# Attention stage: q before k in the transposes of a tile, and P normalized by ScalarE before it is transposed

## The reference, cut to what matters

```python
h = shift_token(x)
q, k, v = split(h @ wqkv, 3)                 # 4096 x 512 each
q = l2norm(q) * q_scale;  k = l2norm(k) * k_scale
q, k = rotary_xpos(q, k)
# every token sees the tokens of the last 256 places (window of three tiles)
sim  = (8 * q) @ k.T, masked                 # per head, 128 x 384 for a tile
attn = softmax(sim)                          # exp, row sum, divide
o    = attn @ v
x    = x + o @ wo
```

## Time and profile before

| | us |
|---|---|
| median of 3 runs | 3535.35 (3533.59 to 3536.51) |
| the profiled execution | 3534.11 |
| its span, first to last instruction | 3532.3 |
| PE busy, of the span | 3269.6 (93%) |
| DVE busy | 1825.5 (52%) |
| ACT busy | 1227.1 (35%) |
| POOL busy | 937.7 (27%) |
| attention stages, by the 64 reciprocals (L1184) | from 354 to 1104 and from 1977 to 2729 |

### The profile page before, as it was taken

How to read it: one execution, slowest core, us unless ns; L and a number is a source line. 1 busy time by engine, 2 the same in 40 slices (tenths; PEclk the granted TensorE clock), 3 DMA queues, 4 the chain that set the end, 5 groups by cost and what they waited for, 6 DMA issues and landing times.

```text
span 3532.3 us, 53670 instructions
## 1 busy us (share of the span) xinstructions
PE 3269.6 (93%) x19880; PEld 2666.5 (75%) x19880; DVE 1825.5 (52%) x3534; ACT 1227.1 (35%) x2445; POOL 937.7 (27%) x1536
## 2 busy tenths in 40 slices
PE   5995999999995999999996899999998799999999
PEld 5884777777774888787774777777776578777787
DVE  2553666666665443333333566666666534333343
ACT  1112555555553111111112555555554211111111
POOL 0004555455454300000001554554553600000000
PEclk9997999999998999999998999999999899999999
DMA  3223111111113211111113101111111411111110
GB/s 115 72 72 130 55 58 55 61 52 37 58 49 91 69 60 60 60 54 60 60 60 130 49 31 60 58 55 60 58 46 52 114 60 60 60 60 60 60 60 30
DMA packets 167415, 225.26 MB, mean 64 GB/s; under 512 B 25032, under 2 KB 94792, under 8 KB 166904
## 3 DMA queue, kind: packets, MB, share of 16 engines
q1 hardware_dynamic: 150264, 205.06, 17.7%
q10 hardware_dynamic: 16896, 16.78, 1.5%
HBM read 131.60 MB, written 60.83 MB: 54 GB/s over the span
## 4 chain that ended last, share of the span: by engine, by line
PE 76%; issue 7%; POOL 7%; DVE 6%; ACT 2%; DMA 1%; SPq 1%; POOLq 0%; DVEq 0%; ACTq 0%
PE bank L311 25%; PE bank L313 23%; PE bank L312 23%; PE bank L694 3%; PE bank L504 2%; POOL a_rt L1421 1%; DVE a_ss L1136 1%; POOL a_rs L1422 1%; POOL a_rt L1419 1%; POOL a_rt L1418 1%; DVE a_V_lo L1164 1%; ACT a_sq L883 1%; PE bank L758 1%; DMA a_stage<-in_L_ffn_wqkv 1%; DVE a_krot L1143 1%
## 5 line engine op out<-in xcount | busy, mean ns | idle before, releaser
L311 PE MATMUL bank<-f_hT_hi,f_w_hi 128*128 128x512 f32 (+1 forms) x1408 | 560.4, 398 | 15.6 <-ACT f_hT_hi L992 15.6
L313 PE MATMUL bank<-f_hT_hi,f_w_lo 128*128 128x512 f32 (+1 forms) x1408 | 558.0, 396 | 0.0
L312 PE MATMUL bank<-f_hT_lo,f_w_hi 128*128 128x512 f32 (+1 forms) x1408 | 557.3, 396 | 0.0
L1332 DVE SCALAR_TENSOR_TENSOR f_uraw<-bank,f_b,f_gate 128x512 f32<-128x512 f32 (+1 forms) x176 | 132.1, 751 | 721.4 <-ACT f_gate L1008 721.2
L1008 ACT ACTIVATE f_gate<-bank,f_b 128x512 f32<-128x512 f32 (+1 forms) x176 | 121.2, 689 | 1008.3 <-PE bank L313 1008.3
L922 ACT ACTIVATE a_P<-a_S,a_bias 128x384 f32<-128x384 f32 x512 | 314.6, 615 | 304.1 <-DVE a_bias L1177 304.1
L1188 DVE TENSOR_TENSOR a_PT_lo<-bank,a_PT_hi 128x768 fp32r<-128x768 f32 x256 | 244.4, 955 | 236.5 <-ACT a_PT_hi L927 236.5
L311 PEld LDWEIGHTS bank<-f_hT_hi,f_w_hi 128*128 128x128 f32 (+1 forms) x1408 | 261.1, 185 | 80.4 <-ACT f_hT_hi L992 16.2
L311 PE MATMUL bank<-a_PT_hi,a_V_hi 128*64 128x128 f32 x1536 | 301.8, 232 | 15.1 <-DVE a_PT_lo L1188 10.7
L313 PEld LDWEIGHTS bank<-f_hT_hi,f_w_lo 128*128 128x128 f32 (+1 forms) x1408 | 261.6, 186 | 67.7
L312 PEld LDWEIGHTS bank<-f_hT_lo,f_w_hi 128*128 128x128 f32 (+1 forms) x1408 | 261.5, 186 | 66.5
(11 more groups left out here) (168 smaller groups left out, 6998.7 us busy)
## 6 DMA issues: line engine op xcount, KB each, us to landing
a_h<-x_layer_in SPq DMA_DIRECT2D x128, 128.0 KB, 2.2
a_res<-x_layer_in SPq DMA_DIRECT2D x64, 256.0 KB, 2.8
x_after_attention<-out_tiles SPq DMA_DIRECT2D x64, 256.0 KB, 2.0
f_h<-x_after_attention ACTq DMA_DIRECT2D x32, 512.0 KB, 4.4
f_res<-x_after_attention SPq DMA_DIRECT2D x64, 256.0 KB, 3.6
f_x<-in_x SPq DMA_DIRECT2D x64, 256.0 KB, 3.6
x_layer_in<-f_res SPq DMA_DIRECT2D x64, 256.0 KB, 2.9
out<-f_res SPq DMA_DIRECT2D x64, 256.0 KB, 3.0
```

Of the source, the lines that this page charges most:

```text
L311: pe.matmul(dst, w[0], m[0], start=start, stop=False)
L312: pe.matmul(dst, w[0], m[1], start=False, stop=False)
L313: return pe.matmul(dst, w[1], m[0], start=False, stop=stop)
L1332: dve.scalar_tensor_tensor(f_uraw[0:ROWS[m], m % 2, :], bank[pair_of(u, m)][0:ROWS[m], :], f_b1[0:ROWS[m], 0, m:m + 1], f_gate[0:ROWS[m], ...
```

## The change

The P of a head is multiplied by its reciprocal row sum on ACT right after the exponential and before its transposes (`normalize`, in place, two heads at a time), in four portions per tile. DVE makes the reciprocals in four portions of two heads (`inverse(x, i)`), into a buffer of two tiles. The widening on POOL, the transposes of the reciprocals on PE, their copy on ACT and the multiplication of PV on DVE are gone. `o_hi` and `o_lo` now read PV from PSUM, in two halves of 64 partitions each.

The transposes of q go to slot B (`q_T`), those of k to slot C (`k_T`); the buffer of the transposed q is doubled, because the next tile's q is now written while the scores of the tile still read it. POOL rotates q ahead of the norms. The orders of ACT and DVE are written anew to match. In addition the transposes wait for other readers of their bank.

```diff
-            a_QT = pair(s, "a_QT", [P, PAIRS, P])
+            a_QT = pair(s, "a_QT", [P, 2, PAIRS, P])
-            a_inv = s("a_inv", [P, H])
+            a_inv = s("a_inv", [P, 2, H])
-            a_inv_wide = s("a_inv_wide", [P, H, HD])
-            a_invT = s("a_invT", [P, PAIRS, P])
-            a_O = s("a_O", [P, PAIRS, P])
 # tensor
+                def q_T(x):
+                    pe.wait_ge(a_q_rotated, START + G + x + 1)
+                    if here(x + 1):
+                        pe.wait_ge(a_hT_lo, START + G + x + 2)
+                    transpose_tile(turn, a_qrot[:]).then_inc(a_QT_mm, 1)
                 def k_T(x):
                     pe.wait_ge(a_k_normed, START + G + x + 1)
-                    if x >= 2:
-                        pe.wait_ge(a_invT_set, START + G + x - 1)
-                    else:
-                        pe.wait_ge(a_hT_lo, START + G + x + 2)
+                    pe.wait_ge(a_QT_hi, START + G + x + 1)
+                    pe.wait_ge(a_QT_lo, START + G + x + 1)
                     transpose_tile(turn, a_krot[:]).then_inc(a_KT_mm, 1)
-                def inv_T(x): ...
                 def p_T(x, i):
-                    pe.wait_ge(a_exp, START + (G + x) * H + 2 * i + 2)
+                    pe.wait_ge(a_P_set, START + (G + x) * H + 2 * i + 2)
                 # step: slot A
-                    if here(t - 1):
-                        inv_T(t - 1)
                 # slot B
-                        k_T(t + 1)
+                        q_T(t + 1)
                 # slot C
-                        q_T(t + 1)
+                        k_T(t + 1)
 # scalar
                 def o_hi(x):
-                    act.wait_ge(a_O_set, START + (G + x + 1) * 2)
-                    act.activation(a_OT[0][:], a_O[:], ACT.Copy).then_inc(a_O_hi, 1)
+                    act.wait_ge(a_PV_mm, START + (G + x + 1) * PAIRS)
+                    for odd in range(2):
+                        act.activation(a_OT[0][odd * HD:odd * HD + HD, :, :], quarters(bank[4 + odd][0:HD, :]), ACT.Copy)\
+                           .then_inc(a_O_hi, 1)
+                def normalize(x, i):
+                    act.wait_ge(a_inv_set, START + (G + x) * PAIRS + i + 1)
+                    for h in (2 * i, 2 * i + 1):
+                        act.activation(a_P[:, h % 4, :], a_P[:, h % 4, :], ACT.Copy, scale=a_inv[:, x % 2, h:h + 1])\
+                           .then_inc(a_P_set, 1)
 # order on ACT after the change:
 # square(0,t+1) q_copy(t+1) exp(t,2) o_hi(t-1) p_T(t,0) exp(t,3) normalize(t,1) value(t+1)
 # exp(t,4) exp(t,5) p_T(t,1) q_T(t+1) normalize(t,2) exp(t,6) exp(t,7) p_T(t,2) k_T(t+1) normalize(t,3)
 # square(1,t+2) k_copy(t+2) exp(t+1,0) exp(t+1,1) p_T(t,3) h_T(t+3) normalize(t+1,0)
 # vector
+                def inverse(x, i):
+                    dve.wait_ge(a_exp, START + (G + x) * H + 2 * i + 2)
+                    dve.reciprocal(a_inv[:, x % 2, 2 * i:2 * i + 2], a_sum[:, x % 2, 2 * i:2 * i + 2]).then_inc(a_inv_set, 1)
-                def o_normed(x): ...
                 def o_lo(x):
-                    dve.wait_ge(a_O_hi, START + G + x + 1)
-                    dve.tensor_tensor(a_OT[1][:], a_O[:], a_OT[0][:], ALU.subtract).then_inc(a_O_lo, 1)
+                    for odd in range(2):
+                        r = slice(odd * HD, odd * HD + HD)
+                        dve.wait_ge(a_O_hi, START + 2 * (G + x) + odd + 1)
+                        dve.tensor_tensor(a_OT[1][r, :, :], quarters(bank[4 + odd][0:HD, :]), a_OT[0][r, :, :], ALU.subtract)\
+                           .then_inc(a_O_lo, 1)
 # order on DVE after the change:
 # sums(0,t+1) mask_max(t,2) mask_max(t,3) o_lo(t-1) p_T(t,0) inverse(t,1) mask_max(t,4) mask_max(t,5) value(t+1)
 # inverse(t,2) p_T(t,1) q_T(t+1) k_norm(t+1) result(t-1) mask_max(t,6) mask_max(t,7) inverse(t,3) p_T(t,2) k_T(t+1)
 # sums(1,t+2) mask_max(t+1,0) mask_max(t+1,1) inverse(t+1,0) p_T(t,3) h_T(t+3)
 # gpsimd
                 def rotate_q(x):
                     pool.wait_ge(a_q_copied, START + G + x + 1)
+                    pool.wait_ge(a_k_rotated, START + G + x + 1)
                 def rotate_k(x):
                     pool.wait_ge(a_k_copied, START + G + x + 1)
+                    pool.wait_ge(a_q_rotated, START + G + x)
-                def widen_inv(x): ...
                 for t in STEPS:
                     if here(t + 1):
+                        rotate_q(t + 1)
                         norms(t + 1)
-                        rotate_q(t + 1)
-                    if here(t):
-                        widen_inv(t)
                     if here(t + 2):
                         rotate_k(t + 2)
```

More of the change, by code:

```diff
@@ L658, in project_out @@
                 def project_out(x):
-                    pe.wait_ge(a_O_hi, START + G + x + 1)
-                    pe.wait_ge(a_O_lo, START + G + x + 1)
+                    pe.wait_ge(a_O_hi, START + 2 * (G + x + 1))
+                    pe.wait_ge(a_O_lo, START + 2 * (G + x + 1))
                     if here(x + 2):
@@ L684, in scores @@
                         r = slice(odd * HD, odd * HD + HD)
-                        three_passes(pe, bank[odd][:, 0:WIN * P], [a_QT[n][r, i, :] for n in range(2)],
+                        three_passes(pe, bank[odd][:, 0:WIN * P], [a_QT[n][r, x % 2, i, :] for n in range(2)],
                                      [a_KT[n][r, i, j * P:(j + WIN) * P] for n in range(2)], True, True)\
@@ L898, in q_T @@
                     act.wait_ge(a_QT_mm, START + G + x + 1)
-                    act.activation(a_QT[0][:], quarters(turn[:]), ACT.Copy).then_inc(a_QT_hi, 1)
+                    act.activation(a_QT[0][:, x % 2, :, :], quarters(turn[:]), ACT.Copy).then_inc(a_QT_hi, 1)
                 def k_T(x):
@@ L943, in attention @@
                         exp(t, 2)
-                        p_T(t, 0)
-                    if here(t - 1):
-                        inv_T(t - 1)
-                    if here(t):
-                        exp(t, 3)
                     if here(t - 1):
                         o_hi(t - 1)
+                    if here(t):
+                        p_T(t, 0)
+                        exp(t, 3)
+                        normalize(t, 1)
                     if here(t + 1):
@@ L953, in attention @@
                     if here(t):
+                        exp(t, 4)
+                        exp(t, 5)
                         p_T(t, 1)
+                    if here(t + 1):
+                        q_T(t + 1)
+                    if here(t):
+                        normalize(t, 2)
+                        exp(t, 6)
+                        exp(t, 7)
+                        p_T(t, 2)
                     if here(t + 1):
@@ L957, in attention @@
                     if here(t):
[L958 to L965, removed]
+                        normalize(t, 3)
                     if here(t + 2):
@@ L970, in attention @@
                         exp(t + 1, 0)
+                        exp(t + 1, 1)
                     if here(t):
@@ L975, in attention @@
                     if here(t + 1):
-                        exp(t + 1, 1)
+                        normalize(t + 1, 0)
             def feed(l):
@@ L1223, in attention @@
                         mask_max(t, 3)
[L1224 to L1228, removed]
                     if here(t - 1):
                         o_lo(t - 1)
+                    if here(t):
+                        p_T(t, 0)
+                        inverse(t, 1)
+                        mask_max(t, 4)
+                        mask_max(t, 5)
                     if here(t + 1):
@@ L1233, in attention @@
                     if here(t):
-                        mask_max(t, 4)
-                        mask_max(t, 5)
+                        inverse(t, 2)
                         p_T(t, 1)
                     if here(t + 1):
-                        k_T(t + 1)
+                        q_T(t + 1)
+                        k_norm(t + 1)
                     if here(t - 1):
@@ L1243, in attention @@
                         mask_max(t, 7)
+                        inverse(t, 3)
                         p_T(t, 2)
                     if here(t + 1):
-                        q_T(t + 1)
-                    if here(t):
-                        inverse(t)
+                        k_T(t + 1)
                     if here(t + 2):
@@ L1253, in attention @@
                         mask_max(t + 1, 1)
+                        inverse(t + 1, 0)
                     if here(t):
```

45 lines of the change are left out of this document (7 added, 38 removed).

## The result

The changed kernel takes 3448.07 us in the median of four executions, beside 3535.93 for the kernel before on the same chip: 87.9 us less. One of the four was a slow one of 6183.74; the other three lie between 3446.30 and 3449.62, with a median of 3446.5, and give the ratio 0.9749, interval 0.9730 to 0.9768. The forecast was 3444. The profiled execution took 3449.62, its span 3447.6 against 3532.3: 84.7 less.

The account below looks back on a forecast made before the run. PE's own list plus its stall for V's low part paced the step: 24.35 - (22.87 + 0.05) = 1.43 us, 83 over 29 steps and 2 stages, 91 with the ends, giving 3444 us; range 3437 to 3470.

Parts of the forecast that it names:

- The floor of 22.87: Attention step on PE: if nothing waits, 3 x 5.83 + 5.38 = 22.87 us, 1.47 less than before.
- a stall of 0.05: Output projection waiting for V's low part: 0.04 to 0.08 us remains of 1.02, taken as 0.05.
- The tight chain: Slot A to B, ACT and DVE: P, normalization of pair 1, then V, with 0.03 to 0.27 us to spare.
- the rival of a late V: Normalization or O's halves dearer, V's high part late on ACT: 0.4 us a step remain, 3464 us; chance 14%.
- The upper bound, from the 768-wide copy: ACT's normalization of pair 1 priced at most 0.81 and 0.71 us, leaving a stall of 0.4 to 0.45.
- DVE's held pair: O's two half-height low-part operations on DVE don't overlap, 3.35 to 4.74 us; P's low part is held behind them too.
- Slot B to C: DVE and POOL: norms at 10.3 us, k's norm 11.0, masks of pair 3 at 12.22, just when ready.
- The slower rival: POOL takes q first and, if stretched, delays k's norm on DVE by 3.8 us: 135 us slower, 3670; chance 4%.
- The steps: Attention stages: 1.43 us saved a step, 29 steps, 2 stages: 83 us.
- The ends: Start and end of the two attention stages: 8 us less, from -2 to 16.

Follow-up runs that it names:

- the exchange alone: Kernel before with q transposed in slot B, k in C, q's rotation ahead of the norms, k's norm later on DVE, P not normalized: 3474.6 us, ratio 0.9821.
- The extra ACT operation: Changed kernel with one more 128x384 copy on ACT between the normalization of pair 1 and V's high part: 3465.9 us, ratio 0.9796.

## Why the prediction was right

**The floor of 22.87.** The forecast step was 22.92, this floor and a stall of 0.05; measured are 22.87 (957.65 to 980.52) and 22.88 in the mean. That the step meets the floor to the hundredth is partly luck: slot A is 0.03 longer than priced, C and D are 0.02 shorter each, and slot B keeps 0.03 of stall. The two halves have been measured apart, the transposes (0.43) and the stall (1.05 by the exchange alone).

**The tight chain.** The walk's times into the step, against the trace: P's high part 3.73, measured 3.82; its low part 4.74, 4.67; end of the second normalization 7.0, 6.85; V's high part 6.9, 6.76; end of V's low part 8.2, 8.18; PE 8.31 to 8.35, measured 8.34. So the stall was 0.03 where 0.05 was priced, and the rival of a late V did not come: the normalization costs 0.608 in the mean and 0.51 from one to the next, priced at 0.60 and 0.50 from the exponential. The upper bound, from the 768-wide copy, was not needed. The extra ACT operation showed that the rival's mechanism was real and only its price absent.

**DVE's held pair.** O's low halves took 1.40 for two of 0.7. The Trainium skill, "VectorE: DVE Perf Modes", section "Two Vector instructions with no wait between them", asked for this, and the trace agrees. That P's low part was held behind them as well is not shown: it started 0.06 after them (962.26 to 962.32), but its high part was itself only there at 962.28. The two copies of O's high part took 1.19 together and put P's high part 0.09 later than the walk had it.

**Slot B to C.** k's norm 11.0, measured 10.73; norms of POOL 10.3, measured 10.23; the result 11.6, 11.36; the masks 12.22, 12.26. The rotation of q runs at 1.28 to 1.30, as forecast. The run with the normalization alone shows the same contention from its other side, k's norm against q's rotation. "GPSIMD Engine Reference", section "Key points" of the Trainium skill, names two SBUF inputs of the DVE operation as the condition; O's low part before and k's norm have them, and the trace agrees. The slower rival needed every POOL operation stretched and had no sign of it.

**The steps** gave 83.8 us (42.2 and 41.6) where the sum had 83.

**The ends.** This is the term of the sum that was off: 8 forecast, 2.8 found in the accounting (1.0 and 1.8 a stage), and 2.0 lost elsewhere, so 3446.5 to 3448 instead of 3444. The waits did shrink (3.55 to 2.16). What the forecast left out is that the time of the matmuls behind them is not fixed: the new tail has three waits of 2.0 to 2.2 us with little PE work between, and the granted clock there is 0.62, against 0.90 before. That the waits bring the clock down is shown by filling them. Why the new tail fell further than the old one, which waits longer, is not shown, and the run of the kernel before with its tail filled says that it can differ from one execution to the next.

With both tails filled the stages of the profiled executions are 46.5 and 46.7 us apart, 93.2 in the two, against 86.7 without; the steps were forecast at 83 of that. The ratios 0.9722 and 0.9983 give 0.9739, which is 92 us of 3538, some 6 us to either side by their intervals. The forecast of 91 agrees with that pair, but a term of 8 us is not confirmed by it alone. The 1.6 us ahead of the first Q projection are not explained; they are under the spread of the runs.

## What to carry to other kernels

- When one engine's list is the floor, walk one step with the times at which that engine wants each input, and price each new operation by the nearest row. The sum of spare times tells more than busy shares: here 0.5 us more on ACT, which was busy for 17.3 of the 22.9 us, cost 0.3 a step.
- A stall can be removed by the order in which slow helpers are fed, not by faster work. The exchange alone gave more than the arithmetic that was saved.
- Where PE waits a few times in a row at the end of a stage, look at the clock behind the waits too, and try to fill them with idle transposes. It gave 8.0 us in the two stages of the changed kernel and 1.5 in those of the kernel before.

## What was not expected of the hardware

- Waits of PE of 2.0 to 2.2 us, three within 18 us, went with a granted clock of 0.62; two of 1.98 and one of 3.55, also within 18 us, with 0.90. One of 2.5 in each step of 27 went with 0.83 in the slot behind it. Filled with transposes: 1.00.
- Two operations on SBUF of the same size, one on DVE and one on POOL: 1.77 beside 1.78 us, instead of 0.69 and 1.29 apart. This was in the rows before; new is that k's norm and q's rotation do the same (1.01 and 1.70) once their order brings them together.
- The same 128x384 product with one number a row takes 0.61 on ACT in the mean and 0.42 in the median on DVE, where the longest took 1.53.
